# One kernel, one change: GpSimd's order of row transfers and powers in the expert stage

## The reference

```python
x = layernorm(x + attention(x))                 # softmax over clipped scores, causal
gate_logits = einsum('bsd,ed->bse', x, gate_w) + gate_b + expert_bias
top_idx = argmax(gate_logits, axis=-1)          # one expert per token
for e in range(8):
    h = relu(x @ w1[e] + b1[e])                 # 128 -> 512
    y = h @ w2[e] + b2[e]                       # 512 -> 128
    out = out + (top_idx == e) * y
x = layernorm(x + out)
```

## Time and profile before

| What | Value |
|---|---|
| median of 3 runs (lowest to highest) | 439.85 us (438.35 to 442.32) |
| the profiled execution, its own time | 439.83 us |
| its span, first to last instruction | 438.1 us |
| time outside the span | 1.73 us |
| busy share of the span: PE, DVE, ACT, POOL | 95%, 83%, 81%, 35% |
| start of the expert stage (first up_rows) | 341.92 us |
| first load of a late tile issued | 381.10 us |
| last write starts | 435.48 us |

### The profile page before, as it was taken

The page is one execution under the profiler, slowest core; times in us unless marked ns, Lnnn a source line. Parts: engine busy times, 40 slices in busy tenths (PEclk is TensorE's granted clock), DMA queues, the critical chain, the costliest instruction groups (busy, mean ns, idle before and its releaser), DMA issues. The chain is left out here.

```text
span 438.1 us, 12324 instructions
## 1 busy us (share of the span) xinstructions
PE 416.3 (95%) x4235; PEld 230.2 (53%) x4235; DVE 362.1 (83%) x824; ACT 356.4 (81%) x568; POOL 152.1 (35%) x164
## 2 busy tenths in 40 slices
PE   8899999999999999999999999998999899699993
PEld 6533344444443444444444444443444698599992
DVE  3978897999998889999987999999878578377764
ACT  3979999999998999998899999998889564376661
POOL 8221001315213013512401314212001466688887
PEclk9889999999999999999999999999899999899998
DMA  5268510668671135544500760674410255477640
GB/s 154 50 167 195 162 49 1 144 145 227 145 170 30 45 87 126 123 112 103 133 2 6 164 149 27 142 170 133 125 39 2 73 140 156 146 223 197 200 136 20
DMA packets 33005, 50.62 MB, mean 116 GB/s; under 512 B 5627, under 2 KB 16545, under 8 KB 32944
## 3 DMA queue, kind: packets, MB, share of 16 engines
q1 hardware_dynamic: 25488, 36.51, 34.1%
q10 hardware_dynamic: 5184, 9.05, 7.3%
q0 software_dynamic: 2272, 4.27, 2.9%
HBM read 21.35 MB, written 5.33 MB: 61 GB/s over the span
## 5 line engine op out<-in xcount | busy, mean ns | idle before, releaser
L1032 ACT ACTIVATE prob<-ring 128x1024 f32<-128x1024 f32 x288 | 274.5, 1039 | 25.8 <-PE ring L1224 25.0
L1242 PE MATMUL o_acc<-prob,v_stat 128*32 128x512 f32 (+3 forms) x1536 | 155.8, 501 | 2.9 <-DVE prob L705 2.1
L1224 PE MATMUL ring<-queries,keys 32*128 32x512 f32 (+3 forms) x1536 | 126.8, 385 | 0.4 <-DVE queries L665 0.4
L1224 PEld LDWEIGHTS ring<-queries,keys 32*128 32x128 f32 x1536 | 71.0, 187 | 71.4 <-issue 48.0
L691 DVE TENSOR_SCALAR prob<-prob 128x2048 f32<-128x2048 f32 x64 | 77.4, 1220 | 7.2 <-ACT prob L1032 6.8
L705 DVE SCALAR_TENSOR_TENSOR prob<-prob,mask_hi 128x1024 f32<-128x1024 f32 (+1 forms) x80 | 82.2, 1028 | 0.0
L1120 ACT ACTIVATE prob<-ring,b1T 128x128 f32<-128x128 f32 x156 | 44.6, 368 | 35.6 <-issue 16.4
L704 DVE TENSOR_SCALAR prob<-prob 128x1024 f32<-128x1024 f32 (+1 forms) x80 | 64.7, 808 | 6.6 <-ACT prob L1032 6.1
L584 POOL DMA_INDIRECT by_expert<-xrow,index x32 | 40.1, 1254 | 78.1 <-DVE index L800 71.0
L1242 PEld LDWEIGHTS o_acc<-prob,v_stat 128*32 128x32 f32 x1536 | 34.1, 109 | 57.2 <-issue 39.5
L565 POOL TENSOR_TENSOR rstd<-var_eps,const 128x4 f32<-128x4 f32 x8 | 16.4, 2048 | 92.0 <-DVE var_eps L748 92.0
(11 more groups left out here) (117 smaller groups left out, 343.5 us busy)
## 6 DMA issues: line engine op xcount, KB each, us to landing
queries<-query_parts SPq DMA_DIRECT2D x60, 256.0 KB, 4.0
v_stat<-in_w ACTq DMA_DIRECT2D x34, 256.0 KB
keys<-key_parts SPq DMA_DIRECT2D x60, 128.0 KB, 2.5
queries<-by_expert SPq DMA_DIRECT2D x39, 66.0 KB
xrow<-in_x_rows SPq DMA_DIRECT2D x8, 264.0 KB, 4.4
xT<-in_x_T SPq DMA_DIRECT2D x8, 256.0 KB, 3.0
v_stat<-in_w SPq DMA_DIRECT2D x5, 256.0 KB
out<-prob,queries POOLq DMA_INDIRECT x39
```

What stands on the lines that cost most here:

```text
L1032: act.activation(prob[u % P_SLOTS][:, 2 * half:2 * half + 2, :].rearrange("p h s -> p (h s)"), slot(("score", u, half))[:], ACT.Exp, scale ...
L1224: last = pe.matmul(out[:, j % 2 * QC + off:j % 2 * QC + off + w], keys[hg][r, kt * P:(kt + 1) * P], queries[hg][r, qc, part, QC - w:QC], s ...
L1242: last = pe.matmul(o_acc[j * VW:(j + 1) * VW, QC - w:QC], v_stat[b % 2][:, hg, kt, j, :], prob[u % P_SLOTS][:, j, off:off + w], start=begi ...
```

## The change

Two things are changed on GpSimd, and VectorE's order follows.

**Routes.** Half 6: four routes stood in one go ahead of the tile loop; now one stands in each of iterations 1, 2, 3 and 4. Half 7: two stood in iteration 9 and two in 10; now one stands in each of 9, 10, 11 and 12.

**Powers.** For tiles 0 to 35 (`PAIRED_TILES` = 36) one power of two columns is taken for two tiles, in each even iteration; it waits for the variance of the second of them. Tiles 36, 37 and 38 keep a power each. The writes of tiles 0 to 34 stand one iteration later than before, and iteration 37 holds two. On VectorE an odd iteration normalises two tiles and an even one none. No arithmetic is changed, and the number of writes and routes is the same: 39 and 32; powers in the tile loop go from 39 to 21.

```diff
-ROUTE_AT = {9: (0, 1), 10: (2, 3)}
+FIRST_ROUTE_AT = {1: (0,), 2: (1,), 3: (2,), 4: (3,)}
+ROUTE_AT = {9: (0,), 10: (1,), 11: (2,), 12: (3,)}
...
+PAIRED_TILES = (TILES - 3) // 2 * 2
...
-        y_var = [sb(f"y_var{i}", [P, 1]) for i in range(2)]
-        y_rstd = [sb(f"y_rstd{i}", [P, 1]) for i in range(2)]
+        y_var = [sb(f"y_var{i}", [P, 2]) for i in range(2)]
+        y_rstd = [sb(f"y_rstd{i}", [P, 2]) for i in range(2)]
...
-            for u in range(B * UB, B * UB + QT):
-                if route_at(u):
-                    route(*route_at(u))
-
-            def y_inverse_std(c):
-                pool.wait_ge(y_vared, c + 1)
-                pool.tensor_tensor(y_rstd[c % 2][:], y_var[c % 2][:], const[:, CONST["half"]][:, 0:1],
+            def y_inverse_std(c, w):
+                t = slice(c % 2, c % 2 + w)
+                pool.wait_ge(y_vared, c + w)
+                pool.tensor_tensor(y_rstd[c // 2 % 2][:, t], y_var[c // 2 % 2][:, t], const[:, CONST["half"]][:, 0:w],
                                    ALU.pow).then_inc(y_rstd_ready, 1)
...
             for c in range(TILES + 2):
-                if 1 <= c <= TILES:
-                    y_inverse_std(c - 1)
-                if c >= 2:
+                if 2 <= c <= PAIRED_TILES and c % 2 == 0:
+                    y_inverse_std(c - 2, 2)
+                if PAIRED_TILES < c <= TILES:
+                    y_inverse_std(c - 1, 1)
+                if 3 <= c <= PAIRED_TILES + 1:
+                    write(c - 3)
+                if c > PAIRED_TILES:
                     write(c - 2)
                 if TAIL_AT.get(c) == "out":
                     inverse_std(LAST_HALF)
+                if c in FIRST_ROUTE_AT:
+                    route(LAST_HALF - 1, FIRST_ROUTE_AT[c])
                 if c in ROUTE_AT:
                     route(LAST_HALF, ROUTE_AT[c])
...
             def y_norm(c):
-                dve.wait_ge(y_rstd_ready, c + 1)
+                dve.wait_ge(y_rstd_ready, c // 2 + 1 if c < PAIRED_TILES else c - PAIRED_TILES // 2 + 1)
...
-                if c >= 2:
+                if 3 <= c <= PAIRED_TILES + 1 and c % 2:
+                    y_norm(c - 3)
+                    y_norm(c - 2)
+                if c > PAIRED_TILES + 1:
                     y_norm(c - 2)
```

5 lines of the change are left out of this document (3 added, 2 removed).

## The result

The changed kernel took 450.7 us (median of 4 runs, 447.25 to 452.04) against 440.97 us of the kernel before beside it: a ratio of 1.0229, 95% interval 1.018 to 1.0278. A later group of runs gave 1.0191 (1.0149 to 1.0234). It is slower by some 2% (whether by more than that the intervals leave open), and outside the range of 438.0 to 446.4 us. The profiled execution took 451.04 us, its span is 449.3 us, 11.2 more than the 438.1 before.

A forecast was written before the change was run, and what follows sets the result against it. The prediction took TensorE's pitch of 1.91 us a tile as the bound, with GpSimd just fast enough. Its terms summed as 439.83 + 0.6 + 0.7 - 0.3 + 1.2 = 442.0 us, range 438.0 to 446.4.

The forecast's parts named there:

- The last half's routes: Change to the late tiles: last route ends at 381.7, TensorE has tile 17 at 385.3, not 384.69; +0.6 us.
- the hold-up: Stretch 372 to 381 before the change: VectorE adds tile 11 only at 381.11, TensorE waits 2.20 us and runs slowly.
- SyncE's step: From the end of the last route to SyncE's load of tile 17: 1.6 us, between 0.9 and 2.36.
- the landing: From the issue of tile 17's load to TensorE having its rows: 2.0 us, between 1.5 and 2.5.
- rival 1: The hold-up recurs ahead of the last routes; tile 17 at 389.5, 4.8 late; 445.5 us; chance 0.22.
- The steady part: Late tiles at 1.91 us each: TensorE hides the some 0.3 us a tile that pairs save; 0.
- The clock: Around turn 17: TensorE idles for rows, then runs slowly at the lower clock; +0.7 us, bounds 0 and 1.4.
- The first half's routes: Start of the tile loop: spread routes may bring back the flip job's 0.76 us; -0.3, between -0.8 and +0.35.
- The end: Power 34+35 to the last write takes 10.18 us, ending at 437.7 instead of 436.47; +1.2 us.
- Rival 2: Bursts of routes caused both hold-ups, spacing removes them; tile 17 1.2 early; 439.8 or 438.6 us; chance 0.23.
- Rival 3: The two-column power costs twice a narrow one, 1.16 instead of 0.74 us; 443.3 us; chance 0.04.
- The port rule: Two VectorE norms in a row hold GpSimd's DMA preparation, at most 0.35 us more each; 443.1 us; chance 0.06.

The follow-up runs named there:

- e_routes_ahead: The changed kernel with the last half's routes ahead of the power and write of their iteration; ratio 1.0153.
- e_last_routes: The kernel before with only the last half's routes spread, one per iteration in 9 to 12; ratio 1.0064.
- e_pairs_last: The changed kernel with the first half's routes back in their bunch ahead of the first power; ratio 1.0166.
- e_spaced: The changed kernel with, from iteration 13, the odd tile's write ahead of the wide power and waiting for VectorE's next sum; ratio 1.0314.
- e_dose: The kernel before with three writes (17, 23, 29) put off to just ahead of the next tile's; ratio 1.0035.
- e_first_routes: The kernel before with only half 6's routes spread, one per iteration in 1 to 4; ratio 1.0012.
- e_norm_each: The changed kernel with both groups of routes as before and one norm in every iteration instead of two in every second; ratio 1.0066.
- e_pairs_write_first: The changed kernel with both groups of routes as before and the odd tile's write ahead of the wide power; ratio 1.0303.

## Why the prediction was wrong, point by point

**The step that failed first** is in "The last half's routes": "The wait for tile 11 inside this chain costs nothing if the hold-up is gone". The hold-up was not gone. The chain of GpSimd's own work was right, 9.11 us by its sum and 10.14 - 1.08 = 9.06 in the trace. But it began 2.7 us later (tile 9's variance ends at 375.16 and not 372.49) and waited 1.08 us for tile 11 (2.56 in the repeat), so the last route ended at 385.4 and not 381.7. SyncE's step took 2.8 us and not 1.6, the landing 1.5 and not 2.0. This is rival 1 in its place: tile 17 at 389.5 by its sum, 389.70 in the trace, though its parts missed both ways, and its time of 445.5 us was some 5 too low. It had a chance of 0.22. e_routes_ahead bears it out in the timeline: with the route taken out of the wait, turn 17 comes 2.4 us sooner (3.4 than in the repeat).

The wait is the smaller part. Of the 4.4 us between the 385.3 of the sum and 389.70, the later start is 2.7, the wait 1.1, SyncE's step 1.2 and the landing -0.5. And where nothing waited for tile 11, the later place of the routes still cost 3.4 us (e_last_routes), 3.6 (e_pairs_last) and 3.7 (e_spaced against e_dose) from down 0 to turn 17, where the sum had +0.6. Two more steps of it explain that. SyncE's step was sized at 1.6 us and took 2.15 or more in every profile. And the 384.69 that the sum was held against was no wait for rows: TensorE came to that turn late by itself, so the 3.59 us behind the issue were no landing, and a cure of the hold-up would have shown a wait (4.91 us in e_dose), not a gain.

**The steady part, taken at 0,** is the second failed step, +2.8 us. The reasoning (TensorE hides all that a pair saves) was right about the saving: the wide power took 0.74 to 0.75 us, as said. It left out that the order of GpSimd's DMAs could go with a cost to those that follow TensorE. Pairs put a write right behind the last one, and with them, on each of the chips with late signals, came three or four slips of some 0.9 us; e_last_routes and e_first_routes, on such a chip without the pairs, have none. On the others e_norm_each kept the pitch; whether the unedited pairs would too wasn't measured. Why a signal is late stays open.

**The clock**, +0.7 between 0 and 1.4: turn 17 to turn 19 took 1.8 us more. The mechanism was right (idle, then the 1.2 GHz level), the term mis-sized: it was bounded by the one slow stretch in the rows of before, which cost 1.4 us. In e_spaced, behind 6.55 us of idle time, turn 17 to turn 19 took 6.8. The Trainium skill, "TensorE: Matmul & The Clock Gate", section "Part 1: The HAM clock gate", has the half rate as the level after idling. The traces agree: the granted clock went to 0.50 within the 6.43 us of idle time in e_last_routes and 1.2 us behind the end of the 2.89 us in the changed kernel.

**The first half's routes**, -0.3: the wait at tile 0 did go (0.04 for 1.29 us behind the product), and nothing was kept. In e_first_routes the gain was gone by tile 7; in the changed kernel and its repeat a late tile 8 came instead. With pairs and last routes these routes cost some 0.3 to 0.6% (1.0191 and 1.0229 against 1.0166, intervals overlapping).

**The end**, +1.2: right. Power 34+35 to the last write was to take 10.18 us and took 10.11, against 8.78.

**The rest.** Rival 2 falls as a whole: in e_first_routes the spread routes left signals late. One half of it is borne out: tile 0's sum was on time with spread routes, and with the last half's spread tile 11's variance started 33.2 us behind down 0 (e_last_routes), not 37.1. But in e_last_routes and e_pairs_last a hold-up stood around tile 14, and neither was faster. On the two other chips tile 0's sum was on time with the routes in a row as well. Rival 3 falls by the 0.74. The port rule (the Trainium skill, "SBUF — State Buffer", section "Terms", on the shared port pair) asked for up to 0.35 us more on a write beside two norms; a write that follows at once took 0.98 to 1.04 us, so the trace doesn't show it. The forecast summed terms one by one. Whether the parts cost more together is not clear of noise (1.6 or 2.0% apart, 2.3 or 1.9% together).

No kernel here beat the one before.

## What to carry to other kernels

Before moving a transfer that others wait for (here the routes that SyncE's loads wait for) behind a wait in a queue, price it with the awaited event where the profile has it, not only where it would be if the stall ahead were gone. And ask whether the engine that receives it is waiting for it in the profile at all: if it is late for a reason of its own, its time says nothing of when the transfer is there. Halving the powers of an engine that hides behind another gained nothing in the middle here and cost 1.5 us at the end, where its last results came a tile later. And when an exchange of two instructions is to put distance between two others, write down the ring of waits (power, norm, write, write: 4.4 us) before the order: what one engine does while the other answers is what an exchange takes away.

## What the runs showed of the hardware that was not expected

By the modelled ends of its rows, TensorE's signals reached ScalarE 0.4 to 1.4 us late in the steady part (up to 5.6 in the early tiles of the kernel before, 6.5 in e_pairs_write_first), at the same three pairs of tiles in repeats on different chips, and from tile 15 on not at all in six of eight profiles on two other chips and once in each of the two others. The kernel before took the same time on all of these chips within 0.6% (438.4 to 441.0 us). In e_last_routes the granted clock fell to 0.50 in the middle of 6.43 us of idle time and stayed there for 5.8 us behind it; behind 2.89 us of idle time in the changed kernel it was 0.50 for 3.4 us.
